# The router folded into the qkv and out layers of a fused perceiver kernel, a new order of steps, and two of four copies of k made by VectorE

## The reference

```python
x = x + softmax(heads(layernorm(x)) @ heads(ctx).T * scale) @ heads(ctx) @ W_out.T + b_out
n = layernorm(x)
ct_q, ct_kv = n @ Wd_q_w + Wd_q_b, n @ Wd_kv_w + Wd_kv_b
query = ct_q @ Wu_q_w + Wu_q_b + rope(ct_q @ Wq_r_w + Wq_r_b)
key   = ct_kv @ Wu_k_w + Wu_k_b + rope(n @ Wk_r_w + Wk_r_b)
value = ct_kv @ Wu_v_w + Wu_v_b
x = x + softmax(query @ key.T / scale) @ value @ Wo_w + Wo_b
n = layernorm(x)
expert = argmax(softmax(n @ Wg + bg))            # one of 8 for each row
x = x + gelu(n @ W1[expert] + b1[expert]) @ W2[expert] + b2[expert]
```

## Time and profile before

| | us |
|---|---|
| median of 3 runs | 849.17 (847.39 to 851.77) |
| profiled execution, its own time | 850.44 |
| its span | 848.6 |
| TensorE busy | 745.6 (88%) |
| VectorE busy | 584.1 (69%) |
| ScalarE busy | 440.4 (52%) |
| GpSimd busy | 323.7 (38%) |
| first product of xout | at 77.68 |
| last product of the rank | at 657.85 |

### The profile page before, as it was taken

One profiled execution on the slowest core, in us unless ns is written; L12 is line 12 of the kernel. 1 busy time (PEld: TensorE's weight loads), 2 busy tenths in 40 slices (PEclk: granted clock), 3 DMA queues, 4 the chain that ended last, 5 costly groups with the idle time before them and its releaser, 6 DMA issues.

```text
span 848.6 us, 26125 instructions
## 1 busy us (share of the span) xinstructions
PE 745.6 (88%) x10442; PEld 552.9 (65%) x10442; DVE 584.1 (69%) x1163; ACT 440.4 (52%) x1095; POOL 323.7 (38%) x638
## 2 busy tenths in 40 slices
PE   5997878989899898988989889898888779999998
PEld 3544756768677685776857667586676646666664
DVE  3467677777767777777777777767535646788883
ACT  2343475564655656556465655646422335555552
POOL 2113453342523424243242432424310444876642
PEclk9998999999899999999999999999998899999999
DMA  9953764665645565465654546442231599554430
GB/s 275 325 151 67 152 158 122 153 149 115 169 115 139 146 144 145 130 152 137 151 139 137 152 120 168 140 114 89 92 133 51 180 372 363 171 161 141 145 114 4
DMA packets 113848, 129.05 MB, mean 152 GB/s; under 512 B 13950, under 2 KB 80766, under 8 KB 113728
## 3 DMA queue, kind: packets, MB, share of 16 engines
q1 hardware_dynamic: 105984, 109.26, 46.8%
q0 software_dynamic: 5520, 16.26, 5.6%
q10 hardware_dynamic: 2224, 1.86, 0.8%
HBM read 114.76 MB, written 14.42 MB: 152 GB/s over the span
## 4 chain that ended last, share of the span: by engine, by line
PE 66%; DVE 9%; POOL 8%; ACT 7%; issue 6%; DMA 4%; SPq 0%; DVEq 0%; POOLq 0%; ACTq 0%
PE bank L507 11%; PE bank L509 9%; PE bank L508 9%; PE bank L1561 7%; PE scores L548 5%; PE bank L572 5%; PE bank L501 4%; PE scores L558 3%; ACT prob L823 3%; POOL operand_lo L1293 2%; PE bank L704 2%; PE scores L1539 2%; PE scores L1541 2%; PE scores L1540 2%; DMA k_block<-in_L_attn_Wu_v_w 2%
## 5 line engine op out<-in xcount | busy, mean ns | idle before, releaser
L823 ACT ACTIVATE prob<-scores,negmax 128x257 f32<-128x257 f32 x256 | 118.2, 477 | 26.4 <-DVE negmax L1031 25.7
L507 PE MATMUL bank<-qkv_hi,operand_hi 128*128 128x396 f32 x256 | 96.0, 375 | 0.0
L1031 DVE TENSOR_REDUCE negmax<-scores 128x2 f32<-128x514 f32 x128 | 82.0, 682 | 15.5 <-PE scores L548 15.5
L1021 DVE STREAM_TRANSPOSE k_t<-keys 128x512 f32<-128x512 f32 x128 | 87.8, 689 | 2.9 <-DMA keys<-in_ctx 2.9
L508 PE MATMUL bank<-qkv_lo,operand_hi 128*128 128x396 f32 x256 | 88.5, 346 | 0.0
L509 PE MATMUL bank<-qkv_hi,operand_lo 128*128 128x396 f32 x256 | 88.0, 344 | 0.0
L1561 PE MATMUL bank<-w_all,hidden 128*128 x184 | 82.8, 593 | 0.6 <-ACT hidden L1614 0.6
L572 PEld LDWEIGHTS bank<-prob_t,context 128*32 128x32 f32 x4096 | 46.6, 115 | 54.1 <-issue 46.6
L558 PE MATMUL scores<-consts,prob 128*128 128x128 f32 x512 | 74.8, 278 | 4.8 <-ACT prob L823 4.7
L1275 POOL COPY plast<-prob 128x2 f32<-128x2 f32 x128 | 24.7, 193 | 129.8 <-ACT prob L823 129.7
L1657 DVE TENSOR_TENSOR w_lo<-w_all,w_hi 128x512 fp32r<-128x512 f32 x89 | 71.6, 863 | 1.8 <-ACT w_hi L1593 1.7
(11 more groups left out here) (244 smaller groups left out, 1671.4 us busy)
## 6 DMA issues: line engine op xcount, KB each, us to landing
keys<-in_ctx SPq DMA_DIRECT2D x256, 128.0 KB, 4.4
context<-in_ctx SPq DMA_DIRECT2D x64, 512.0 KB, 4.6
w_all<-in_L_ffn_W SPq DMA_DIRECT2D x16, 1024.0 KB, 12.1
b<-in_L_ffn_b SPq DMA_DIRECT2D x23, 256.0 KB, 3.5
norm_scratch<-norm SPq DMA_DIRECT2D x16, 256.0 KB, 2.0
x_tile<-in_x SPq DMA_DIRECT2D x8, 256.0 KB, 5.5
x_pair<-in_x SPq DMA_DIRECT2D x8, 256.0 KB, 5.5
x_scratch<-x_tile SPq DMA_DIRECT2D x8, 256.0 KB, 3.0
```

Source lines behind the costliest of these rows:

```text
L507: pe.matmul(to, op_hi[op][:, c, :], w_hi[name][:, c, columns], start=(c == 0), stop=False)
L823: act.activation(prob[pair][:, gg, :], scores[:, g, 0:J], ACT.Exp, bias=negmax[b % 2][:, g:g + 1], accum_out=sums[t % 2][:, g, bl:bl + 1]) ...
L1021: dve.transpose(dst, src).then_inc(keys_turned, 1)
L1031: dve.tensor_reduce(negmax[b % 2][:, 2 * pair:2 * pair + 2], scores[:, 2 * pair:2 * pair + 2, 0:J], AX.X, ALU.max, negate=True).then_inc(m ...
```

## The change

**The router.** The step of the set-up adds three kinds of unit: `center` takes the mean over rows off Wg, `turned` transposes Wo, and `gate` multiplies Wo with the centred Wg and sums Wg with the out bias. The result becomes 8 more columns of the out weights, the centred Wg 8 more of the qkv weights. qkv's product then has the router's share of normed x1, which GpSimd scales back by the deviation (`gate_keep`, two small operations), and out's product has the share of the self attention. Out with its 520 columns does not fit into one bank of 512: each of its four parts is two halves of 260 columns in two banks, so 24 products instead of 12. VectorE adds the two shares (`gate_sum`), and the choice multiplies by the deviation. The turn of norm3, its move to `x3` and the gate's product are gone; norm3 is still made and stored for the experts.

**k's placement.** Of the four copies onto k_block's diagonal, ScalarE makes two and VectorE two.

**The steps and banks.** Nearly all constants are new; which bank a stage uses too. `TURN3`, `X3_MOVE` and `GATE` are gone, `GATE_KEEP` is new.

The diff, cut to its core:

```diff
-AV, SELF_HI, SELF_LO, OUT, X2, ROOT3 = 66, 66, 70, (81, 85, 86, 87), 89, 85
+AV, SELF_HI, SELF_LO, OUT, X2, ROOT3 = 63, 73, 71, (86, 88, 92, 94), 96, 99
...
-ACT_K = (0, 1, 2, 3)
+ACT_K = (1, 3)
+OUT_BANK = 1
...
+GATE_AT = 3 * D + ROT
+QKV_W = GATE_AT + E
 QW = QKV_W // 4
+HALF, GH = D // 2, E // 2
...
+         + [("center", 0)] + [("turned", c) for c in range(G)] + [("gate", 0)])
...
+        def out_part(c):
+            hi, lo = out_weights(w_hi, c), out_weights(w_lo, c)
+            for half in range(2):
+                pe.matmul(out_pair[:, half, 0:HALF + GH], op_hi[OP_SELF][:, c, :], hi[:, half, :], start=(c == 0), stop=False)
+            for half in range(2):
+                pe.matmul(out_pair[:, half, 0:HALF + GH], op_hi[OP_SELF][:, c, :], lo[:, half, :], start=False, stop=False)
+            for half in range(2):
+                done = pe.matmul(out_pair[:, half, 0:HALF + GH], op_lo[OP_SELF][:, c, :], hi[:, half, :], start=False, stop=(c == G - 1))
+            return done
...
+            if kind == "center":
+                until.wait_ge(tables_loaded, 32)
+                until.wait_ge(small_loaded, 16 * SMALL)
+                for g in range(G):
+                    done = pe.matmul(bank[:, 0:E], tables[:, P:2 * P], wg[:, g, :], start=(g == 0), stop=(g == G - 1))
+            if kind == "turned":
+                until.wait_ge(staged_a_loaded, 32)
+                for k in range(G):
+                    done = pe.transpose(bank[:, k * P:(k + 1) * P], staged_a[:, k, c * P:(c + 1) * P], ident)
+            if kind == "gate":
+                until.wait_ge(centered, 2)
+                until.wait_ge(wo_turned, G)
+                for o in range(G):
+                    for k in range(G):
+                        pe.matmul(bank[:, o * E:(o + 1) * E], wo_t[:, k, o * P:(o + 1) * P], wg[:, k, :], start=(k == 0), stop=(k == G - 1))
+                for k in range(G):
+                    done = pe.matmul(bank[:, G * E:(G + 1) * E], tables[:, P:2 * P], wg_bias[:, k, :], start=(k == 0), stop=(k == G - 1))
...
-            t = tile_at(step, TURN3, LATER["TURN3"])
-            if t >= 0:
-                bank = bank_for("norm3", t)
-                until.wait_ge(normed_r, t + 1)
-                turn(norm3, bank, norm3_turned)
-            t = tile_at(step, GATE, LATER["GATE"])
-            if t >= 0:
-                if t >= T - 2:
-                    fill(BEFORE["GATE"])
-                bank = bank_for("gate", t)
-                until.wait_ge(x3_moved, t + 1)
-                until.wait_ge(small_loaded, 16 * SMALL)
-                for g in range(G):
-                    done = pe.matmul(bank[:, 0:E], x3[:, g * P:(g + 1) * P], wg[:, g, :], start=(g == 0), stop=(g == G - 1))
-                done.then_inc(gate_done, 1)
...
-            t = tile_at(step, X3_MOVE, LATER["TURN3"])
-            if t >= 0:
-                until.wait_ge(norm3_turned, t + 1)
-                until.wait_ge(gate_done, t)
-                if t == 0:
-                    until.wait_ge(unit_done, len(UNITS))
...
+                until.wait_ge(gate_kept, t + 1)
+                until.wait_ge(gate_used, t)
+                dve.tensor_tensor(halves(gate_sum[:, :]), halves(gate_x1[t % 2][:, :]), out_pair[:, :, HALF:HALF + GH], ALU.add)
+                dve.tensor_tensor(halves(x_tile[t % 4][:, :]), halves(x_tile[t % 4][:, :]), out_pair[:, :, 0:HALF], ALU.add).then_inc(x2_made, 1)
                 until.wait_ge(x2_made, t + 1)
                 until.wait_ge(rstd_r, t)
                 measure(x_tile[t % 4][:, :], "r", measured_r)
...
-                until.wait_ge(gate_done, t + 1)
+                until.wait_ge(rstd_r, t + 1)
+                until.wait_ge(x2_made, t + 1)
                 until.wait_ge(small_loaded, 16 * SMALL)
                 until.wait_ge(dve_own, own.count)
-                dve.tensor_tensor(logits[:, :], banks[bank_of["gate"]][:, 0:E], bias_g[:, :], ALU.add).then_inc(gate_used, 1)
+                dve.scalar_tensor_tensor(logits[:, :], gate_sum[:, :], rstd["r"][:, :], bias_g[:, :], ALU.mult, ALU.add).then_inc(gate_used, 1)
...
+            t = tile_at(step, GATE_KEEP)
+            if t >= 0:
+                until.wait_ge(qkv_moved, 4 * t + 4)
+                until.wait_ge(x2_made, t - 1)
+                until.wait_ge(weight_lo, len(CUTS))
+                until.wait_ge(pool_own, own.count)
+                a = own.done(pool.tensor_scalar(gate_x1[t % 2][:, :], v_w[t % 2][:, D:D + E], std_s[:, :], None, ALU.mult))
+                until.wait_ge(pool_own, a)
+                pool.tensor_tensor(gate_x1[t % 2][:, :], gate_x1[t % 2][:, :], gate_c[:, :], ALU.add).then_inc(gate_kept, 1)
```

More of the change, by code:

```diff
@@ L282, in program @@
     inv_t = staged_c[:, 0, :]
-    low_wide = x3[:, :].rearrange("p (k n) -> p k n", k=G)
+    low_wide = soft[:, :].rearrange("p (k n) -> p k n", k=G)
+    wo_t = staged_b
     row_uq, row_uk, last_rows = norm_w, norm3, soft
     scores = ctx.enter_context(nc.psum_tensor("scores", [P, G, 512], F32))
-    psum = [ctx.enter_context(nc.psum_tensor(f"bank{i}", [P, 512], F32)) for i in range(4)]
-    att_bank, banks = psum[0], psum[1:4]
+    att_bank = ctx.enter_context(nc.psum_tensor("att_bank", [P, 512], F32))
+    stage_banks = ctx.enter_context(nc.psum_tensor("stage_banks", [P, 3, 512], F32))
+    banks = [stage_banks[:, i, :] for i in range(3)]
+    out_pair = stage_banks[:, OUT_BANK:OUT_BANK + 2, :]
     def by_head(t_):
@@ L385, in program @@
     emptied = {"queries": queries_placed, "xout": x1_made, "norm": norm_lo, "q": q2_moved, "self": soft_shifted, "av": self_lo,
-               "out": x2_made, "norm3": x3_moved, "gate": gate_used, "rank": rank_used}
+               "out0": x2_made, "out1": x2_made, "rank": rank_used}
     last_bank = banks[(bank_of["queries"] + 1) % 3]
@@ L808, in set_up @@
                 cut(w_hi["qkv"][:, c, K_AT:K_AT + D], staged_d[:, c, :])
+            if kind == "turned":
+                until.wait_ge(unit_done, n + 1)
+                act.activation(wo_t[:, c, :], bank[:, :], ACT.Copy).then_inc(wo_turned, 1)
+            if kind == "gate":
+                until.wait_ge(unit_done, n + 1)
+                cut(gate_columns(w_hi), bank[:, 0:G * E].rearrange("p (c h e) -> p c h e", c=G, h=2))
         def move_prob(b, pair):
@@ L949, in scalar_program @@
                 until.wait_ge(staged_a_loaded, 32)
-                cut(w_hi["out"][:, step - OUT_CUT_AT, :], staged_a[:, step - OUT_CUT_AT, :])
+                cut(out_weights(w_hi, step - OUT_CUT_AT)[:, :, 0:HALF], halves(staged_a[:, step - OUT_CUT_AT, :]))
+            if step == GATE_CUT_AT:
+                until.wait_ge(centered, 1)
+                cut(w_hi["qkv"][:, :, GATE_AT:QKV_W], wg[:, :, :])
             stages(step)
@@ L1240, in vector_program @@
                 c = step - OUT_CUT_AT
-                cut("out", c, w_lo["out"][:, c, :], staged_a[:, c, :], w_hi["out"][:, c, :])
+                cut("out", c, out_weights(w_lo, c)[:, :, 0:HALF], halves(staged_a[:, c, :]), out_weights(w_hi, c)[:, :, 0:HALF])
+            if step == GATE_CUT_AT:
+                cut("norm_gate", 0, w_lo["qkv"][:, :, GATE_AT:QKV_W], wg[:, :, :], w_hi["qkv"][:, :, GATE_AT:QKV_W])
             if step == BIAS_END_AT:
@@ L1258, in root @@
             pool.tensor_scalar(shift[n][:, :], rstd[n][:, :], mean_var[n][:, 0:1], -1.0, ALU.mult, ALU.mult).then_inc(done, 1)
+            if n == "s":
+                own.done(pool.tensor_scalar(std_s[:, :], mean_var[n][:, 1:2], EPS, rstd[n][:, :], ALU.add, ALU.mult))
         def rotated_columns(dst, src):
```

140 lines of the change are left out of this document (84 added, 56 removed).

## The result

Over nine runs each on the same chip the changed kernel takes 841.93 us (837.37 to 844.26), the kernel before 849.40 (846.16 to 851.77): a ratio of 0.9905, with a 95% interval of 0.9879 to 0.9930. It is faster, by 0.9%, where 2.9% was forecast. The profiled execution has a span of 839.1 us (before 848.6). All times are medians of the runs in a kernel's usual state; a run at 2148 us is left out of `e3_k_by_scalar`.

What follows compares the result with a forecast made beforehand. TensorE was taken to set the pace, busy 31.19 of 35.16 us per tile. 850.4 + 5.5 (set-up) - 23 (tile loop) - 5.9 (last tile) = 827, median 1.3 lower, stated as 825 us; range 815 to 835, chance 0.50.

Steps and rivals of the forecast that it cites:

- From qkv to the last attend: Tile stretch from qkv to the last attend: 17.0 us with no wait, where it was 17.9.
- The walk: Following the new order once around a tile with the old durations: 33.5 us instead of 35.16.
- rival 1: Tile loop: ScalarE's prob move and exps each 0.6 us later, a tile gains only 0.45; 842 us, chance 0.18.
- 4: Tile loop: out's narrow records cost 0.18 us each, 1.44 us a tile more; 845 us, chance 0.06.
- the late points: Tile loop: ScalarE's prob move ending at 4.5 us and the exps with the move at 12.5, after the last attend.
- The work per tile: TensorE's work in each tile: norm3 turn and gate removed, narrower out records and wider qkv added; net -1.22 us.
- The waits: TensorE's waits in each tile, new order: 0.7 and 1.8 us after xout, 0.5 at qkv; 0.4 us less wait.
- rival 3: Tile loop: short waits after xout lower TensorE's clock, costing 2.6 us a tile or more; 853 to 863 us, chance 0.07.
- Set-up: Before the first xout: making the folded router matrix delays xout from 77.68 to 83 us, +5.5, bounds 0 and +10.
- Last tile: Last tile, nothing beside it: shorter k path, no norm3 turn and an earlier choice of expert; together -5.9 us.
- (a): Last tile, turned k: no wait for the v move's bank, copies split over two engines; -2.4 us.
- (b): Last tile: the norm3 turn between the parts of out goes; -0.5 us.

Runs made afterwards that it cites:

- e3_k_by_scalar: e1 with all four copies of the turned k made by ScalarE, as in the kernel before; 833.27 us, ratio 0.9778.
- e1: Changed kernel with SyncE's keys load issued four steps earlier, ahead of the x load and the norm3 store; 833.27 us, ratio 0.9801.
- e2: e1 with norm3 made and stored three steps later, behind the prob move and norm_w on ScalarE; 828.48 us, ratio 0.9727.
- E7: e1 with the set-up product that folds the router cut from 40 records to 10; 826.75 us, ratio 0.9724.

## Why the prediction was wrong

**The step that failed.** "From qkv to the last attend ... 17.0. I find no wait in it." In tiles at full clock of the changed kernel this stretch takes 17.9 to 19.6 us, 18.6 on average, and VectorE waits 1.8 to 3.5 us for keys in it; in e1 it is 17.2. The walk took TensorE, VectorE, ScalarE and GpSimd around the tile and left SyncE out. The change moves norm3 from 33 us into a tile to 7 us into the next, and with it two operations of SyncE's queue that wait for it, one of them, the x load, not touched by the diff. The keys load stands behind both, at 7.8 us, and VectorE wants the keys at 12.5. That the tile would be "above 34.5 at clock 1.00" was named as the mark of rival 1 or 4; it was neither. That rival 1 names 842 us, the time measured, is chance: the late points that it speaks of, on ScalarE, are where the walk put them within 0.4 us. E1 gives back 8.7 us in the median and 10.5 of the 12.2 missing in the loop.

**The work per tile.** Forecast -1.22; in e1, where no wait cuts the groups, 29.91 against 31.19: -1.28. Right.

**The waits.** The walk had 0.7 and 1.8 behind xout and 0.5 at qkv; measured 0.98, 1.44 and 0.30. Xout to qkv takes 11.47 (walk 11.1), the end of the last attend to xout 4.99 (5.4). Right within 0.4, and the chains are made of what the walk says: with norm3 behind the prob move the 1.44 becomes 0.74.

**The clock.** The forecast kept the dips of before. They came in five of twelve full tiles (before six), but in the changed kernel they did not add to the time that the late keys cost. The 38 us of rival 3 never threatened there. In e2, with shorter tiles, its dips did come in ten of twelve, at 1.3 to 1.8 us each and not the 2.6 of the rival.

**Set-up.** +6.1 against +5.5, inside the bounds, but the closeness is luck: two terms were off in opposite directions. ScalarE's last copy (k_block) ended at 75.03, not 77.6. The product of 40 records then took from 75.18 to 82.45, 7.3 us and not 4.6, since the granted clock was 0.61 from 75.00 to 82.50. E7 confirms that the first xout follows the product.

**First tile.** Forecast unchanged, measured 35.32 against 34.13: +1.2. TensorE waits 2.56 us for ScalarE's prob_t before the second xout there. I have not tested the cause; the wait is in every run (2.06 us in e3, which has no copies of k on VectorE).

**Last tile.** -5.1 against -5.9. From the last statistics to rank it is 648.01 - 643.34 = 4.67, where it was 7.67: the -3.0 forecast. The rest, from xout to the statistics, gave -2.1 and not -2.9. Up to self it gave -3.0 (21.63 us against 24.61), more than the 2.4 of (a). What is missing is in the stretch of (b), from AV to the statistics: 8.98 us instead of 8.18, at a granted clock of 0.81. At 1.00, in e3, it takes 7.63, and that is the 0.5 less of the forecast.

**The sum.** +6.1 - 10.8 - 5.1 + 0.3 = -9.5 us of span. With e1's loop (-21.3) in it, it is -20.0, near the forecast of -23.4 for the profiled execution.

## What to carry to other kernels

When an operation is moved, list everything that waits for its result on every queue, including lines that the diff does not touch, and then what stands behind each of them: here an x load that had always found norm3 done became the gate of a keys load two operations behind it. If a tile at full clock takes no less time than one with a dip, look for something outside TensorE, a transfer that arrives late for example, and ask in each tile which of the two sets its length. And after a wait is taken away, read the clock again: the next gain may be given back there, and a few idle products in the waits can hold it, if they are shorter than the wait.
